# Cross attention in units of four heads with resident keys, and a feed-forward that no longer divides by the sums

## The reference, cut to what matters

```
scores = q @ k.T / sqrt(32)          # 2048 x 154 for a batch and a head
scores = masked where the key is padding or (causal) key > query
out    = softmax(scores) @ v         # then rows @ Wo.T + bo + x
```

## Time and profile before

| | |
|---|---|
| median of three runs | 3451.21 us (3448.59 to 3453.72) |
| the profiled execution, its time | 3448.84 us |
| its span in the trace | 3446.9 us |
| PE busy (matmul) | 3077.2 us, 89% |
| DVE busy | 2216.5 us, 64% |
| ACT busy | 1609.8 us, 47% |
| POOL busy | 1745.6 us, 51% |
| self attention, roughly | 325 to 2135 us |
| cross context | 2389 to 2433 us |
| cross attention | 2435.4 to 2852 us |
| feed-forward with shared experts | 2852.6 to 3220 us |

### The profile page before, as it was taken

The page is one execution under the profiler, slowest core; times in us unless marked ns, Lnnn a source line. Parts: engine busy times, 40 slices in busy tenths (PEclk is TensorE's granted clock), DMA queues, the critical chain, the costliest instruction groups (busy, mean ns, idle before and its releaser), DMA issues. The chain is left out here.

```text
span 3446.9 us, 44367 instructions
## 1 busy us (share of the span) xinstructions
PE 3077.2 (89%) x15510; PEld 1769.8 (51%) x15510; DVE 2216.5 (64%) x4046; ACT 1609.8 (47%) x2933; POOL 1745.6 (51%) x701
## 2 busy tenths in 40 slices
PE   7997999999999999999999994896499994888578
PEld 6875444444444544444444441784255553666433
DVE  4334788888888888888888871563366663666322
ACT  2221466666666666666666664231145451222111
POOL 0001378787887878888788886000200002444255
PEclk9998799999999999999999997997699997999679
DMA  4546445646346464464645344696544444432631
GB/s 173 182 170 176 108 100 110 132 92 151 85 107 147 89 150 95 101 141 101 150 86 110 75 92 121 179 243 163 137 123 123 123 123 138 147 146 110 216 86 34
DMA packets 195323, 442.85 MB, mean 128 GB/s; under 512 B 32618, under 2 KB 60202, under 8 KB 175532
## 3 DMA queue, kind: packets, MB, share of 16 engines
q1 hardware_dynamic: 171014, 295.73, 29.3%
q0 software_dynamic: 24128, 144.75, 19.9%
HBM read 187.47 MB, written 126.04 MB: 91 GB/s over the span
## 5 line engine op out<-in xcount | busy, mean ns | idle before, releaser
L652 DVE TENSOR_REDUCE part_max<-ps_s 128x1 f32<-128x512 f32 x2048 | 1270.1, 679 | 309.9 <-PE ps_s L553 309.9
L749 ACT ACTIVATE probs<-ps_st 128x512 f32<-128x512 f32 x2048 | 1086.4, 600 | 546.0 <-PE ps_st L572 531.6
L511 POOL TENSOR_TENSOR added<-added,probs 128x2048 f32<-128x2048 f32 x256 | 1182.5, 4619 | 91.1 <-ACT probs L749 64.7
L553 PE MATMUL ps_s<-k_stack,q_stack 96*128 96x512 f32 x2048 | 841.9, 427 | 28.3 <-POOL max_parts L501 20.6
L572 PE MATMUL ps_st<-q_stack,k_stack 98*128 98x512 f32 x2048 | 857.2, 424 | 6.6 <-ACT probs L749 5.4
L572 PEld LDWEIGHTS ps_st<-q_stack,k_stack 98*128 98x128 f32 x2048 | 386.6, 189 | 504.6 <-ACT probs L749 363.1
L583 PE MATMUL ps_pv<-probs,v_sb 128*32 128x512 f32 x4096 | 546.5, 606 | 0.0
L553 PEld LDWEIGHTS ps_s<-k_stack,q_stack 96*128 96x128 f32 x2048 | 395.5, 193 | 214.5 <-DVE part_max L652 143.7
L519 POOL DMA_DIRECT2D probs<-probs x128 | 112.8, 881 | 230.8 <-PE ps_pv L583 218.2
L1626 POOL MEMSET e_bias_rows<- 128x1024 f32 x1 | 1.0, 953 | 370.0 <-POOLq L46 370.0
L511 POOL TENSOR_TENSOR added<-probs 128x2048 f32<-128x2048 f32 x32 | 146.3, 4571 | 48.7 <-ACT probs L749 48.7
(11 more groups left out here) (269 smaller groups left out, 3684.6 us busy)
## 6 DMA issues: line engine op xcount, KB each, us to landing
probs<-probs POOLq DMA_DIRECT2D x128, 1024.0 KB, 7.1
xq_stack<-q_parts SPq DMA_DIRECT2D x66, 384.0 KB
q_stack<-q_hi SPq DMA_DIRECT2D x64, 256.0 KB
k_stack<-k_hi SPq DMA_DIRECT2D x64, 256.0 KB, 10.7
q_parts<-q_h_out SPq DMA_DIRECT2D x64, 256.0 KB, 4.9
x_in<-in_x_rows SPq DMA_DIRECT2D x8, 1024.0 KB
q_hi<-qk_h_out SPq DMA_DIRECT2D x8, 1024.0 KB
q_lo<-qk_l_out SPq DMA_DIRECT2D x8, 1024.0 KB, 6.4
```

Source lines behind the costliest of these rows:

```text
L511: pool.tensor_tensor(added[:, w % 2], left, probs[:, k % RING], ALU.add).then_inc(added_up, 1)
L553: pe.matmul(ps_s[:, place % BANKS], q_stack[0:ROWS, w % 4, j, t * P:(t + 1) * P], k_stack[0:ROWS, w // BPB, j, n * BLK:(n + 1) * BLK], sta ...
L652: dve.tensor_reduce(part_max[:, s:s + 1], ps_s[:, (w * SLOTS + s) % BANKS], AX.X, ALU.max)\
L749: act.activation(probs[:, k % RING, j], ps_st[:, n % BANKS], ACT.Exp, scale=SCALE).then_inc(item_used, 1)
```

## The change

Cross attention works in 32 units of four heads by 512 queries. The stacked keys of both batches and all values are loaded once and stay (`kt_stack` for transposed scores, `ks_stack` for scores; the latter has a row with the padding bias, which a row of ones in the query tile adds, so that later blocks need no mask matmul). The loops over blocks are written out. The order on each engine is fixed by hand: in iteration u TensorE does eight times (t = 0 to 7) a transposed-scores tile of unit u and a slot (two tiles) of scores of unit u+2, and before t = 3 turns the maxima of u+1, multiplies the values of u-1 and makes the sums of u-2 (`totals`). Maxima are split into two parts on VectorE (`max_rows`: a copy and a subtraction) and copied as rows by ScalarE, four heads in four instructions. GpSimd adds the two halves of the probabilities of each unit (`add`), and in units 1 to 6 does one step each of splitting the weights ahead. VectorE inverts the sums in PSUM and multiplies. The output is stored normalised. The feed-forward loses the sums, their inverse and the scaling; `cross_context` stores values without ones and one version of each mask.

```diff
@@ class Ahead
-    def split(self, pool):
-        pool.wait_ge(self.loaded, 16 * len(self.weights))
-        for _, raw, high, _ in self.weights:
+    def split_step(self, pool, step):
+        n = step // 2
+        _, raw, high, low = self.weights[n]
+        if step % 2 == 0:
+            pool.wait_ge(self.loaded, 16 * len(self.weights))
             pool.tensor_copy(high, raw).then_inc(self.high_done, 1)
-        for n, (_, raw, high, low) in enumerate(self.weights):
+        else:
             pool.wait_ge(self.high_done, n + 1)
             pool.tensor_tensor(low, raw, high.bitcast(F32), ALU.subtract).then_inc(self.low_done, 1)
...
@@ cross_attention, SP
+                sp.wait_ge(ones_set, 2)
+                load_q(0)
+                load_k(0)
...
+                load_q(1)
+                sp.dma_start(v_sb[:], xv_rows).then_inc(v_loaded, 16)
+                load_q(2)
+                load_q(3)
+                load_k(1)
                 ahead.load(sp)
...
@@ cross_attention, GpSimd
+                for n, (tile, value) in enumerate(((q_stack[ROWS:TOP + 1].bitcast(F32), 1.0), (ks_stack[ROWS:TOP + 1].bitcast(F32), 0.0),
+                                                   (kt_stack[ROWS:TOP].bitcast(F32), 1.0), (mk[:], 0.0),
+                                                   (max_parts[:].bitcast(F32), 0.0), (ones[:], 1.0))):
...
+                def add(u):
+                    pool.wait_ge(item_used, item(u, TILES - 1) + 1)
+                    if exists(u - 2):
+                        pool.wait_ge(dens_done, u - 1)
+                    pool.tensor_tensor(added[:, u % 2], probs[:, u % 2, 0], probs[:, u % 2, 1], ALU.add).then_inc(added_up, 1)
+
+                for u in range(UNITS):
+                    add(u)
+                    if 1 <= u <= ahead.STEPS:
+                        ahead.split_step(pool, u - 1)
...
@@ cross_attention, TensorE
+                def scores(u, s):
+                    j, half = s // 2, s % 2
+                    place = u * SLOTS + s
+                    if place >= BANKS:
+                        pe.wait_ge(max_done, place - BANKS + 1)
...
+                def turn_max(u):
+                    n = turn_item(u)
+                    pe.wait_ge(max_low, u + 1)
...
+                def totals(u):
+                    pe.wait_ge(added_up, u + 1)
+                    if u:
+                        pe.wait_ge(normalized, u)
+                    for j in range(HEADS):
+                        mm = pe.matmul(ps_d[j * HD:(j + 1) * HD], ones[:], added[:, u % 2, j], start=True, stop=True)
+                    mm.then_inc(dens_done, 1)
...
+                for u in range(UNITS + 2):
+                    for t in range(TILES):
+                        if t == BEFORE_TURN:
+                            if exists(u + 1):
+                                turn_max(u + 1)
+                            if exists(u - 1):
+                                weighted_values(u - 1)
+                            if exists(u - 2):
+                                totals(u - 2)
+                        if exists(u):
+                            transposed_scores(u, t)
+                        if exists(u + 2):
+                            scores(u + 2, t)
...
@@ cross_attention, VectorE
+                def max_rows(u):
+                    parts = max_parts[:].rearrange("p t (j c) -> p j t c", j=HEADS)
+                    dve.wait_ge(max_done, (u + 1) * SLOTS)
+                    if u:
+                        dve.wait_ge(item_done, turn_item(u - 1) + 1)
+                    dve.tensor_copy(parts[:, :, :, 0], neg_max[:, u % 2]).then_inc(max_high, 1)
+                    dve.wait_ge(max_high, u + 1)
+                    dve.tensor_tensor(parts[:, :, :, 1], neg_max[:, u % 2], parts[:, :, :, 0].bitcast(F32), ALU.subtract)\
+                       .then_inc(max_low, 1)
...
+                for u in range(UNITS + 3):
+                    for s in range(SLOTS):
+                        if exists(u + 2):
+                            slot_max(u + 2, s)
+                        if exists(u - 3) and s < 2:
+                            invert(u - 3, s + 2)
+                        if exists(u - 3) and s == 2:
+                            normalize(u - 3)
+                        if exists(u - 2) and 3 <= s < 5:
+                            invert(u - 2, s - 3)
+                    if exists(u + 2):
+                        max_rows(u + 2)
...
@@ cross_attention, ScalarE
+                def max_rows(u):
+                    n = turn_item(u)
+                    act.wait_ge(item_done, n + 1)
+                    for j in range(HEADS):
+                        mm = act.activation(q_stack[ROWS:TOP, u % BUFS, j], ps_st[j * HD:j * HD + 2, n % BANKS], ACT.Copy)
+                    mm.then_inc(item_used, 1)
...
@@ shared_feed_forward
-                sp.dma_start(sums_sb[:], sums.rearrange("h (n k) -> (h n) k", k=BLK)).then_inc(sums_loaded, 16)
-                load_rows(0, 0)
+                load(0, 0)
...
-                sp.wait_ge(inv_made, 1)
-                sp.dma_start(inv_sums.rearrange("h (n k) -> (h n) k", k=BLK), inv_sb[:]).then_inc(inv_stored, 16)
-                sp.wait_ge(inv_stored, 16)
-                load_sums(0, 0, 0)
-                load(1, 0, 1)
+                load(1, 1)
...
-                def scale(i, u):
-
+                def add_bias(i, u):
                     pool.wait_ge(loaded[u], i * (16 * LOADS) + 16 * LOADS)
-                    pool.tensor_tensor(a_raw[:, u], a_raw[:, u], a_inv[:], ALU.mult).then_inc(scaled, 1)
                     for t in range(TPB):
                         pool.tensor_tensor(x_in[:, u, t], x_in[:, u, t], bo_all[:], ALU.add).then_inc(bo_added, 1)
```

More of the change, by code:

```diff
@@ new lines, in slots @@
+                def slots(u, first, end):
+                    for s in range(first, end):
+                        slot_max(u, s)
+                dve.wait_ge(consts_loaded, 80)
+                dve.tensor_copy(ident_r[:], ident[:]).then_inc(ident_ready, 1)
+                dve.wait_ge(ones_set, 6)
+                for u in range(2):
+                    slots(u, 0, SLOTS)
+                    max_rows(u)
+                for u in range(UNITS + 3):
+                    for s in range(SLOTS):
+                        if exists(u + 2):
[8 more added lines that the diff above has]
+                        max_rows(u + 2)
@@ new lines, in raw_out @@
+                def raw_out(u):
+                    if u >= 2:
+                        act.wait_ge(normalized, u - 1)
+                    act.wait_ge(pv_done, u + 1)
+                    act.activation(attn_raw[:, u % 2], ps_pv[:], ACT.Copy).then_inc(raw_done, 1)
+                act.wait_ge(ones_set, 6)
+                act.wait_ge(consts_loaded, 80)
+                max_rows(0)
+                for u in range(UNITS + 1):
+                    for t in range(TILES):
+                        if t == BEFORE_TURN:
+                            if exists(u + 1):
+                                max_rows(u + 1)
+                            if exists(u - 1):
+                                raw_out(u - 1)
+                        if exists(u):
+                            exponentials(u, t)
```

413 lines of the change are left out of this document (183 added, 230 removed).

## The result

The changed kernel takes 3560.34 us (median of four, 3557.86 to 3563.09) where the kernel before takes 3449.9 us beside it: ratio 1.0321, interval 1.0308 to 1.0334. It is slower, as forecast, but by 110 us and not by 24, and above the range. The span of the profiled execution is 3559.5 us against 3446.9, +112.6. Its mean granted TensorE clock is 0.884 against 0.943.

What follows compares the result with a forecast made beforehand. The new loop was taken as bound by passing through four engines in turn, none full, with VectorE held behind GpSimd. Terms -3 + 8.5 + 59 + 1 - 22.8 - 19 = +24 on 3448.8 gave 3475 us, range 3405 to 3530.

Steps and rivals of the forecast that it cites:

- rival A: The forecast itself: VectorE held in each cross-attention unit, TensorE's clock full nearly always; 3445 to 3505 us; chance 0.62.
- rival B: VectorE held, and 3.7 us of TensorE idle time lowers its clock: up to 4.6 us a unit, 3525 to 3575; chance 0.13.
- the hold: In `max_rows`, VectorE's copy waits behind GpSimd's `add`, from about 4.35 to 8.37 us in each unmasked unit.
- 13.05: Forecast us for an unmasked cross-attention unit with VectorE held and TensorE at full clock; 22 full turns, 287 us.
- 455: Forecast us for cross attention from first scores to last output, against 396 before: +59.
- 13.8 and 14.3: Forecast us a unit with causal mask, the second where the scores two units ahead are masked too; 8 units, 112.
- Rival C: Hold avoided because `add` starts after `max_rows` has passed: unit 9.2 us, stage 328, in all 3345 us; chance 0.15.
- the five terms around the stage: Outside the cross-attention loop: earlier stage start -3, first scores +8.5, leaving +1, feed-forward entry -22.8, its steady state -19 us.
- Splitting units: Units 1 to 6: weight splits behind GpSimd's adds hold VectorE's subtraction once more; 16 us, bounds 11 and 23.
- Start: Stage's first memset to first scores, through memsets and 3.1 MB of loads: 26 us against 17.6, +8.5, bounds +4 and +14.
- Entry: Feed-forward start to first projection without sums' reload and scaling, constants late next: 14.3 us against 37.1, -22.8.
- Steady state: Feed-forward without GpSimd's scaling: `norm`'s first two tiles shorten by 3.2 us in six blocks; -19, bounds -10 and -21.

Runs made afterwards that it cites:

- addition later: Changed kernel with one wait added, so GpSimd's add starts only when VectorE has written the maxima parts of the unit two ahead: 3412.67 us.
- TensorE given work: Changed kernel, hold kept, with 12 extra overwritten matmuls of 512 columns in TensorE's idle time before the maxima are turned: 3495.19 us.
- The early start: Later addition and 128 rows, with first loads not waiting for memsets, VectorE doing half of these, first scores waiting only for what they read: 3334.6 us.

## Why the prediction was wrong, point by point

**The step that failed** is "clock full nearly always" of rival A, and behind it the sentence on rival B that made the clock a matter of the 3.7 us of idle time and gave it 0.13. The units of the runs, put side by side, tell what hold and clock cost (unmasked units, us from output to output):

| | clock high | mixed | clock 0.50 |
|---|---|---|---|
| not held | 9.26 (128 rows) | | 12.46 (addition later) |
| held | 12.84 (TensorE given work) | 13.66 (128 rows) | 15.73 (the changed kernel) |

The lower clock costs 15.73 - 12.84 = 2.9 us a held unit and 3.2 a free one; the hold costs 3.3 at the lower clock and 3.6 at the higher. The table puts versions with extra work or padding beside each other, so these prices are good to some tenths of a us. Against 13.05 the unit lost 2.7 us, which over 22 units is 59 of the 88.7 us by which the stage missed its 455. Of the rest, some 15 us lie in six steps around the masked units of the second batch, 13.89 to 17.78 us where the forecast had 13.8 and 14.3; what remains is not divided further. The direct measure is the changed kernel with 128 rows and the hold kept: 3492.14 us instead of 3560.34, inside the forecast's range.

**Why the clock is low** has two parts that the runs separate. (1) With the values contracted over 77 rows, TensorE's clock falls to 0.50 in unmasked units behind waits of at most 0.94 us, and stays there for 120 us without any idle time; widening the eight value matmuls of a unit or adding mask matmuls lifts it. The forecast counted a 77-row matmul as it counts any other and never asked what had changed in the kind of matmul. The rows could have prompted it: the matmuls of the earlier trace rows have 96 rows or more, the values 128, and the clock beside them in the earlier trace rows is 1.00. (2) The wait behind the hold lowers it by itself, as rival B said: the clock falls behind each wait of 3.48 us with 128 rows. Alone that costs 13.66 - 12.84 = 0.8 us a unit, where B had up to 4.6. With 77 rows as well, the clock doesn't come back within the unit. Why it depends on the rows, and on what else beside them, is not shown.

The Trainium skill, TensorE: Matmul & The Clock Gate, Part 1, section What's actually happening, has the gate follow how busy the array has been. The fall behind each wait of 3.48 us agrees. The 120 us at 0.50 with TensorE busy throughout do not, and there the measurement decides.

**The hold** was right in place, cause and size. VectorE's copy begins 0.18 us into GpSimd's addition (0.6 forecast at full clock; 0.79 at 2637.99 in the held kernel with 128 rows), lasts 4.38, TensorE waits 3.0. At the lower clock the margin shrinks, but not to nothing. The Trainium skill, GPSIMD Engine Reference, section Specifications, names VectorE instructions with two SBUF inputs or in a 2-port mode. The subtractions held in the splitting units have two SBUF inputs and agree. The copy has one and is held too; that would agree if it ran in a 2-port mode, which no run here shows. A reduction with one SBUF input is not held (0.18 us).

**Rival C**, the hold avoided, was worked out as a unit of 9.2 us, a stage of 328 and 3345 us. With later addition and 128 rows the chip gives 9.26, 328.4 and 3345.73. The working of the loop was sound; only the chip's clock had to be provided for. That the total agrees to a microsecond is partly luck: the five terms around the stage each missed by 1 to 4 us in the changed kernel, and their sum by 0.3. A slip without effect: the forecast adds TensorE's work in a unit to 7.4 us, its terms give 7.7.

**Splitting units.** Copy and subtraction are held in turn, as forecast; all six subtractions together lose 14.4 us, where the forecast had 16.

**Start.** 29.8 us instead of 26, inside its bounds: the memsets ahead of the first load took 11.1 (11.3 forecast). What comes last is the landing of the last of five constant loads at 2460.02: it is issued at 2448.36, behind the queries and keys and behind one more memset, that of the mask tile, which ends at 2447.97 and for which SP also waits. The early start shows how much of it was order: 12.2 us from the first memset to the first scores.

**Feed-forward.** Entry: what is late next are the constants, as named. They landed 11.1 us after the start, where the earlier trace rows had 10.3, and a_l took 3.24 instead of 2.62, so 17.4 and not 14.3. Steady state: first two tiles of `norm` at 2.05. The row's -22.7 against -19 lies beyond the bound of -21, but it covers all that follows. From the first projection to the first load of the selected experts (3233.8 before, 3349.3 after) the gain is 19.8 us, as forecast; the other 2.9 lie in the selected experts, which were not changed, and their cause was not looked for.

**The range** held no case for a clock that falls without idle time; B alone at its worst (3575) was left outside.

## What to carry to other kernels

Count a matmul's rows, not only its columns and its time, and look at the granted clock: padding a contraction from 77 rows to 128 with zeros cost no matmul time and gave 67 us here (3412.67 to 3345.73), since it kept TensorE's clock up. It isn't a rule for every kernel: narrowed to 77 rows, the kernel before took 3451.69 us against 3448.91. If TensorE is busy throughout and its granted clock is 0.50, more work of another kind may be faster than less. A tiny VectorE copy on the critical path must not meet a long GpSimd instruction: order the long one behind it, or write the copy as a reduction, 148 to 150 us here.

## What the runs showed of the hardware that was not expected

- TensorE stayed at clock 0.50 for 120 us in which it was never idle, with 77-row value matmuls of 32 columns; 24 more matmuls in a unit made it faster (12.46 to 10.08 us).
- The same narrowing in the kernel before left the clock at 1.00 once it was there. In one execution it took TensorE some 27 us of work without a gap to get there from 0.50, in another, on the same instructions, about 5.
- VectorE's one-input copy from SBUF to SBUF, 16 elements a lane, was held 4.38 us by GpSimd's addition; a one-input reduction of the same elements took 0.18 beside it.
- Between two GpSimd instructions a held VectorE can get in or not: a subtraction of 0.19 us slipped in at 2613.31 ahead of an addition that waited for the one before it; at 2524.12, behind a split that waited for nothing, it took 4.39 us.
